# A recurrence on one core: the input quantiser computed in the projection, and matmuls that nobody reads in TensorE's waits

## The reference, cut to what matters

```python
# recurrence, one step a chunk, the state (W_in, W_out) carried on
def step(carry, xs):
    k_h = softmax(einsum('blhd,bDhd->blhD', k_t, W_in)) * lr_t[..., 1:]
    q_h = softmax(einsum('blhd,bDhd->blhD', q_t, W_in))
    o_t = einsum('bqhD,bDhd->bqhd', q_h, W_out) + einsum('bhqk,bkhd->bqhd', qk, v_t)
    W_out = W_out + einsum('bnhD,bnhd->bDhd', k_h, v_t)
    for _ in range(2):            # both states, by attention over the chunk
        ...
# the other way
scale = max(act_scale, 1e-05)
x_int = clip(round(x / scale), -127, 127)
x_dq  = nan_to_num(x_int * scale, nan=0.0, posinf=10000.0, neginf=-10000.0)
y     = einsum('bsi,oi->bso', x_dq, ternary_weight - 1) + bias
```

## Time and profile before

| | us |
|---|---|
| median of 3 runs | 953.45 |
| the 3 runs | 952.24, 953.45, 964.16 |
| the profiled execution | 961.29 |
| its span, first to last instruction | 959.6 |
| mean granted clock of TensorE over the span | 0.784 of 2.4 GHz |

### The profile page before, as it was taken

One profiled execution on the slowest core, in us unless ns is written; L12 is line 12 of the kernel. 1 busy time (PEld: TensorE's weight loads), 2 busy tenths in 40 slices (PEclk: granted clock), 3 DMA queues, 4 the chain that ended last, 5 costly groups with the idle time before them and its releaser, 6 DMA issues. The chain is left out here.

```text
span 959.6 us, 19016 instructions
## 1 busy us (share of the span) xinstructions
PE 674.0 (70%) x6860; PEld 516.7 (54%) x6860; DVE 645.9 (67%) x1809; ACT 341.3 (36%) x794; POOL 377.0 (39%) x513
## 2 busy tenths in 40 slices
PE   1577687788766656899999882154598771696785
PEld 1266465566545535777777682143476551353564
DVE  3763888878857573877777743836554664887886
ACT  1654111111121344666666531211113441475221
POOL 1450444444431454455655055516602662023312
PEclk9988766655669685999999997557757996597895
DMA  2000000000000400120000243364372533100000
GB/s 53 1 1 12 3 2 2 3 2 3 3 2 6 72 0 6 41 77 9 8 8 14 64 132 119 73 97 116 90 179 60 164 108 110 34 0 1 6 17 22
DMA packets 66289, 41.27 MB, mean 43 GB/s; under 512 B 11888, under 2 KB 64192, under 8 KB 66208
## 3 DMA queue, kind: packets, MB, share of 16 engines
q1 hardware_dynamic: 62432, 32.43, 14.2%
q0 software_dynamic: 3776, 7.78, 2.3%
HBM read 26.72 MB, written 13.47 MB: 42 GB/s over the span
## 5 line engine op out<-in xcount | busy, mean ns | idle before, releaser
L1733 ACT ACTIVATE l1a_weights<-l1a_score,l1a_low_top 128x128 f32<-128x128 f32 (+1 forms) x256 | 90.4, 425 | 37.9 <-DVE l1a_low_top L1765 33.9
L1765 DVE TENSOR_REDUCE l1a_low_top<-l1a_score 128x2 f32<-128x512 f32 (+1 forms) x96 | 66.1, 688 | 53.4 <-PE l1a_score L1642 52.4
L1597 POOL TENSOR_TENSOR l1a_q_of<-l1a_q_rows,l_quad_of 128x1024 fp32r<-128x1024 f32 x32 | 59.9, 1895 | 38.0 <-ACT l1a_q_rows L1722 38.0
L1277 POOL DMA_INDIRECT l_done<-l2e_done,l2r_rows x47 | 45.1, 959 | 59.3 <-DVE l2e_done L2482 58.7
L1788 DVE COPY l1a_weightsT<-l1a_flip 128x512 f32<-128x512 f32 x96 | 65.3, 680 | 0.8 <-PE l1a_flip L1677 0.7
L1639 PE MATMUL l1a_score<-l1a_k_rows,l1a_q_of 128*128 128x128 f32 (+1 forms) x256 | 53.2, 313 | 17.9 <-ACT l1a_weights L1733 10.5
L1677 PE MATMUL l1a_flip<-eye,l1a_weights 128*128 128x128 f32 x384 | 59.3, 278 | 0.1
L1639 PEld LDWEIGHTS l1a_score<-l1a_k_rows,l1a_q_of 128*128 128x128 f32 x256 | 38.4, 201 | 33.0 <-ACT l1a_weights L1733 20.5
L1677 PEld LDWEIGHTS l1a_flip<-eye,l1a_weights 128*128 128x128 f32 x384 | 47.4, 145 | 3.1 <-issue 0.8
L827 POOL TENSOR_TENSOR l0s_shared<-l0s_own,l0s_grown 128x512 f32<-128x512 f32 x16 | 18.1, 1132 | 75.3 <-ACT l0s_grown L817 75.3
L1260 POOL DMA_INDIRECT l_rows<-l2r_sent,l2r_slot x32 | 31.9, 998 | 28.6 <-DVE l2r_slot L1244 16.1
(11 more groups left out here) (545 smaller groups left out, 1968.2 us busy)
## 6 DMA issues: line engine op xcount, KB each, us to landing
l2e_wgu<-in_l_wgu SPq DMA_DIRECT2D x47, 128.0 KB, 2.1
l1e_w<-in_l_w SPq DMA_DIRECT2D x46, 128.0 KB, 2.1
l_rows<-l2r_rows SPq DMA_DIRECT2D x1, 3055.0 KB, 19.5
l2e_wd<-in_l_wd SPq DMA_DIRECT2D x47, 64.0 KB, 2.1
l2r_rows<-l_rows SPq DMA_DIRECT2D x3, 780.0 KB, 7.1
l2e_mixed<-l_done SPq DMA_DIRECT2D x8, 256.0 KB, 4.7
l_rows<-l1r_rows SPq DMA_DIRECT2D x1, 1483.5 KB, 11.6
l1r_rows<-l_rows SPq DMA_DIRECT2D x3, 387.0 KB, 3.7
```

What stands on the lines that cost most here:

```text
L1277: self.core.nc.gpsimd.indirect_dma_start(self.done_dram, bass.IndirectOffsetOnAxis(ap=self.rows[:, j, D:D + 1].bitcast(I32), axis=0), done ...
L1597: nc.gpsimd.tensor_tensor(q_of[i][:, 4 * g:4 * g + 4, :], rep(q_rows[:, g, :], 1, 4), rep(lat.quad_of[:, 0, 0:4], 2, L), ALU.mult).then_in ...
L1733: last = nc.scalar.activation(weights[s % 2][:, n * width:(n + 1) * width], score[s % 2][:, n * width:(n + 1) * width], ACT.Exp, bias=low_ ...
L1765: nc.vector.tensor_reduce(low_top[:, s % 2, 0:len(heads)], score[s % 2][:, :].rearrange("p (h k) -> p h k", k=key_tiles * P), AX.X, ALU.ma ...
```

## The change: what it does

The quantiser leaves the scan. `l0_project` gets the scale by a transfer of its own, and VectorE quantises there in four pieces of 512 columns: one after `invert(0)`, one after `invert(1)`, two at the end of its program. In `l0_scan` `quantise` and `choose` are gone, as are the transfer of the scale and the two instructions that prepare it. In the scan's TensorE program `fill` adds ten float32 matmuls to a chunk, 128x128 by 128 columns of `xnT`, into columns of a PSUM bank that no one reads: one at the chunk's head, two ahead of the "own" add, two ahead of the "out" add, one ahead of the scores of "in", and four ahead of the "in" add. The first of them has a new wait, for ScalarE's copy of "grown".

```diff
-def l0_project(core, fast):
+def l0_project(core, fast, act_scale_dram):
...
+            @block.sync
+            def _(sp):
+                sp.dma_start(scale[:, :], act_scale_dram.partition_broadcast(P)).then_inc(scale_in, 16)
...
+                def quantise(c):
+
+                    quant = fast.quant[:, c * CH:(c + 1) * CH]
+                    order.then(nc.vector.tensor_scalar(level[:, :], core.xnT[:, c * CH:(c + 1) * CH], inv[:, :], ROUND, ALU.mult, ALU.add))
+                    order.then(nc.vector.tensor_scalar(level[:, :], level[:, :], -ROUND, LEVELS, ALU.add, ALU.min))
+                    order.mark(nc.vector.tensor_scalar(spare[:, :], level[:, :], -LEVELS, scale[:, :], ALU.max, ALU.mult))
+                    order.then(nc.vector.tensor_scalar(quant, level[:, :], LIMIT, LIMIT, ALU.mult, ALU.min))
+                    order.mark(nc.vector.tensor_scalar(finite[:, :], spare[:, :], 0.0, 0.0, ALU.mult, ALU.is_equal))
+                    order.then(nc.vector.tensor_scalar_max(quant, quant, -LIMIT))
+                    order.then(nc.vector.copy_predicated(quant, finite[:, :], spare[:, :]))
...
                 invert(0)
+                dve.wait_ge(scale_in, 16)
+                order.then(nc.vector.tensor_scalar_max(scale[:, :], scale[:, :], 1e-5))
+                order.then(nc.vector.reciprocal(inv[:, :], scale[:, :]))
+                quantise(0)
                 normalise(0, K)
                 invert(1)
+                quantise(1)
                 normalise(1, Q)
+                quantise(2)
+                quantise(3)
...
+                def fill(count, bank=grown_ps):
+
+                    for _ in range(count):
+                        nc.tensor.matmul(bank[:, 3 * P:4 * P], core.eye[:, :], core.xnT[:, 0:P], start=True, stop=True)
...
                     if c:
+                        pe.wait_ge(grown_kept, c)
+                        fill(1)
                         pe.wait_ge(here_ready, c)
...
                         give_results(c - 1)
+                    fill(2)
                     pe.wait_ge(ready["own"], c + 1)
...
+                    fill(2)
                     pe.wait_ge(ready["out"], c + 1)
...
                     last.then_inc(out_summed, 1)
+                    fill(1)
                     pe.wait_ge(old_ready, c + 1)
...
                     if c < LAST:
+                        fill(4, out_ps)
                         pe.wait_ge(ready["in"], c + 1)
...
-                    quantise(c)
                     dve.wait_ge(out_summed, c + 1)
                     mask(w_old, OLD).then_inc(old_ready, 1)
...
-                    choose(c)
                     if c >= 2:
                         sum_squares(c - 2)
```

More of the change, by code:

```diff
@@ L374, in l0_project @@
         rate_wide = sb("rate_wide", [P, NCK, 8, CK])
+        scale, inv, level, spare = sb("scale", [P, 1]), sb("inv", [P, 1]), sb("level", [P, CH]), sb("spare", [P, CH])
+        finite = local.enter_context(nc.sbuf_tensor("l0p_finite", [P, CH], I32))
+        LEVELS, ROUND, LIMIT = 127.0, 1.5 * 2.0 ** 23, 1e4
         near, far = (local.enter_context(nc.psum_tensor(f"l0p_{n}", [P, BANKS, CH], F32)) for n in ("near", "far"))
@@ L386, in l0_project @@
         norms_drawn, rates_drawn = core.sem("l0p_norms_drawn"), core.sem("l0p_rates_drawn")
-        dve_order, pool_order = core.sem("l0p_dve_order"), core.sem("l0p_pool_order")
+        dve_order, pool_order, scale_in = core.sem("l0p_dve_order"), core.sem("l0p_pool_order"), core.sem("l0p_scale_in")
         def four_chunks(toks, s):
@@ L595, in _, with l0_scan @@
                 invert(0)
+                dve.wait_ge(scale_in, 16)
+                order.then(nc.vector.tensor_scalar_max(scale[:, :], scale[:, :], 1e-5))
+                order.then(nc.vector.reciprocal(inv[:, :], scale[:, :]))
+                quantise(0)
                 normalise(0, K)
                 invert(1)
+                quantise(1)
                 normalise(1, Q)
-def l0_scan(core, fast, w_gate_dram, w_out_dram, ternary_dram, bias_dram, act_scale_dram):
+                quantise(2)
+                quantise(3)
+def l0_scan(core, fast, w_gate_dram, w_out_dram, ternary_dram, bias_dram):
     nc = core.nc
@@ L641, in l0_scan @@
         turned = pair("turned", [P, 2, P])
[L642 to L645, removed]
+        bias, mean, square = sb("bias", [P, D]), sb("mean", [P, H]), sb("square", [P, H, HD])
         w_ps = ps("w", [P, 4, CH])
@@ L667, in l0_scan @@
         dve_order, pool_order = sem("dve_order"), sem("pool_order")
-        tern_in, scale_in, bias_in, later_in = (sem(n) for n in ("tern_in", "scale_in", "bias_in", "later_in"))
+        tern_in, bias_in, later_in = (sem(n) for n in ("tern_in", "bias_in", "later_in"))
         out_done, centred, squared = sem("out_done"), sem("centred"), sem("squared")
@@ L687, in _ @@
             def _(sp):
-                sp.dma_start(scale[:, :], act_scale_dram.partition_broadcast(P)).then_inc(scale_in, 16)
                 sp.dma_start(fast.tern_int[:, :], ternary_dram).then_inc(tern_in, 16)
@@ L889, in mask @@
                                                    rep(rep(fast.w_mask[:, :, :].rearrange("p h i -> p (h i)"), 1, 2), 1, 4), ALU.mult)
[L891 to L903, removed]
                 def centre(c):
@@ L938, in _ @@
                         order.mark(nc.vector.tensor_scalar_add(fast.w_tern[:, :], fast.tern_int[:, :], -1.0))
-                        dve.wait_ge(scale_in, 16)
-                        order.then(nc.vector.tensor_scalar_max(scale[:, :], scale[:, :], 1e-5))
-                        order.then(nc.vector.reciprocal(inv[:, :], scale[:, :]))
                     if c >= 2:
                         centre(c - 2)
-                    quantise(c)
                     dve.wait_ge(out_summed, c + 1)
@@ L3012, in build @@
             layer_norm(core, "l0_norm", core.x, core.xn, core.xnT, LN_EPS, loads=[fast])
-            l0_project(core, fast)
-            l0_scan(core, fast, io["l0_w_gate"], io["l0_w_o"], io["l0_ternary"], io["l0_bias"], io["l0_act_scale"])
+            l0_project(core, fast, io["l0_act_scale"])
+            l0_scan(core, fast, io["l0_w_gate"], io["l0_w_o"], io["l0_ternary"], io["l0_bias"])
             l0_finish(core, fast)
```

## The result

The changed kernel takes 948.07 us in the median of 20 runs (940.79 to 956.23), the kernel before 956.22 beside it (20 runs, 951.11 to 964.16): the ratio is 0.9898, 95% interval 0.9872 to 0.9925. The ratios of this document leave out runs over 1.5% above the fastest of their kernel (here one, 956.23); medians and ranges have all runs. The change gains 1.0%, some 8 to 10 us, where 20 were forecast; 948.07 also lies above the range. The profiled execution is the fastest of the 20, 940.79 us.

The account below looks back on a forecast made before the run. The prediction took the scan to be bound by the loop through the engines, not by one engine. Its sum was 961.3 - 21.4 + 0.9 = 940.8 us for the profiled execution; against the median it took 934, range 926 to 946.

Parts of the forecast that it names:

- I take it that the clock stays at 2.4 GHz through the scan: Scan: the fills' full-array work keeps TensorE's granted clock near 1.00, against 0.61 on the mean before.
- about 10.5: Scan's regular chunks: each falls from 11.84 us to about 10.5, some 19 us in all.
- fast, but with gaps: Scan: rival in which the clock falls in two or three chunks, 4 us each; 941 to 945, chance 0.17.
- slower: Scan: rival in which fills delay awaited matmuls at 1.2 GHz, 2.6 us a slow chunk; about 970, chance 0.05.
- eight slow chunks: Scan: the "slower" rival's count, 8 of 14 chunks slow as now, 21 us on top of 949.
- +0.9: Scan's head: the scan starts 0.9 us later, behind the last two quantiser pieces of the projection.
- last chunk 1.9: Scan's end: D, A and half of "grown" save 0.96 + 0.18 + 0.8 = 1.9 us.
- The projection: Projection: a quantiser piece takes 3.5 us; the first two are hidden, the last two end at 92.5.
- G and A's 5 us less to gain: Scan: faster runs may already have more 2.4 GHz, so gain up to 5 us less, 937 at most.

Follow-up runs that it names:

- fills alone: Kernel before with the ten fills added, quantiser left in the scan: 971.07 us, ratio 1.019 to the kernel before.
- the move alone: Changed kernel without its fills, quantiser in the projection: 954.2 us, ratio 1.000 to the kernel before; cut after layer 1, 316.43 us.
- both changes: Changed kernel with last quantiser piece at the head of the scan and each fill as four 32x32 matmuls: 938.85 us, ratio 0.9797 to the kernel before.
- fills at the barrier: Kernel with both changes, cut after layer 1, plus eight small fills behind the scan's last matmul: 296.54 us against 297.59 without them.
- cut programs: Kernels with layers 2 to 4 left out and the state stored: kernel before 316.39 us, changed kernel 307.27 us.
- last piece moved: Changed kernel with its last quantiser piece moved to the head of the scan's VectorE program: 946.85 us, ratio 0.9886 to the kernel before.
- small fills: Changed kernel with each fill as four 32x32 matmuls side by side: 948.6 us, ratio 0.9877 to the kernel before.

## Why the prediction was wrong

The step that failed is "I take it that the clock stays at 2.4 GHz through the scan", with the two terms that stand on it outside the 14 chunks.

- *The steady chunk, "about 10.5"*: right. Twelve of 14 chunks are 10.49, with each term where it was put: the quantiser's place now ends with TensorE, and the fills at the higher clock delay no awaited matmul. That it is the fills that raise the clock is shown: 0.61 before, it is 0.86 with fills alone and 0.55 to 0.62 with the move alone. That the higher clock pays only with the quantiser out of the way is shown too.
- *The clock in the loop*: the two slow chunks cost 0.75 and 3.0 us. That is the mechanism of the rival "fast, but with gaps", which I gave 0.17 and 941 to 945, at 4 us a slow chunk. The prices of the "slower" rival hold where its condition does: 1.34 us for the fills ahead of "own" and "out", measured 1.5 (3.90 us from the transposed "out" to the mask in the slow chunk, 2.42 with the move alone); 1.30 for the four ahead of "in", measured 1.26 with the fills alone. In the changed kernel's slow chunk that second part is 0.6 (the add could start at 237.91 and starts at 238.53), since the clock rises while the four run. What was wrong is the count of eight slow chunks.
- *The head, "+0.9"*: the start was 0.7 later, as priced, but I costed a later start only, not what TensorE's doubled idle time at the barrier goes with. In six traces with two pieces ahead of the barrier TensorE stands 1.9 us, and in five of them the clock falls 0.6 to 2.5 us behind the scan's first matmul; in the eight others, among them all five with the piece moved behind the barrier, it stands 0.93 and the clock falls 6.2 us or more behind it. Moving the piece thus takes both away; by what path the longer idle time brings the fall is not shown. The first mask is 3.9 us late against 0.2 in the sum: 3.7 lost.
- *The end, "last chunk 1.9"*: it gave 0.8, and `l0_finish`, for which the sum had nothing, took 2.2 us more. In the kernel before the clock is up again at 283, ahead of that stage, and low in it only from 286 to 289 (0.93 over 284 to 307). In the changed kernel it is low from 265 to 279 and again from 286 to 288 (0.80 over 272 to 297.3). The first low stretch, with the matmuls of 512 columns, costs some 0.7 us up to the first gated product; the second costs 1.5, where the product with `w_o` takes 2.84 us, not 2.05. That this loss is the clock's is shown on the kernel with both changes: with fills at the barrier the clock is 1.00 throughout and the stage takes 21.9 us, as in the kernel before.
- *The projection*: right. A piece took 3.3 to 3.4 us (priced 3.5), the first, beside GpSimd's draws, 4.7 and still hidden.
- *The baseline*: the sum was put against a profiled execution and then carried over to the median. The spread between runs, for which I allowed "up to G and A's 5 us less to gain", is hardly the scan's: layer 1 alone spreads over 1.1 us.

Summed on layer 1: 20.5 forecast, less 3.6 in the loop (18.8 against 15.2), 3.7 at the head, 3.3 at the end, is 9.9; measured are 9.8 in the profiled pair, from which the parts are taken, and 9.1 in the cut programs.

## What to carry to other kernels

Price a change that lives on TensorE's clock in three stretches, not one: the steady loop, its entry and its exit, since each barrier at which TensorE idles longer can take back what the loop gained. Test the halves of such a change apart: here the move alone and the fills alone gave 0 and a loss of 1.9%, and the pair gained 1%. When whole runs scatter more than the effect, cut the program behind the changed stage before arguing about a few us.

## What the runs showed of the hardware that was not expected

**A later stage has two speeds.** In seven whole programs layers 2 to 4 took either 641.8 to 641.9 us (changed kernel, last piece moved, both) or 652.1 to 652.5 (the four others), with the same code and nothing between. Nearly all of the difference, 9.7 of 10.7 us in this pair, arises in one place, 400 to 420 us behind the end of layer 1. Windows there, changed kernel, then kernel before:

```profile
697.30:707.30 10.00, 9.89 (x50) 7.31 (x49) 5.78 (x18) 1.12 (x3) 0.00 (x0) 0.90 1.00 243
707.30:717.30 10.00, 7.68 (x43) 6.34 (x41) 4.87 (x19) 5.03 (x13) 1.91 (x2) 0.75 0.15 47
```

```profile
707.10:717.10 10.00, 10.00 (x34) 7.74 (x34) 5.71 (x13) 0.74 (x2) 0.00 (x0) 0.50 1.05 257
717.10:727.10 10.00, 10.00 (x32) 7.24 (x31) 1.96 (x7) 0.74 (x2) 0.00 (x0) 0.50 0.00 0
```

TensorE is busy all of the time at the lower clock and the clock does not rise; in the other execution it has. Of the 20 runs of the changed kernel seven lie at 940.8 to 944.2 and eleven at 946.5 to 951.3, which fits two such speeds; what decides between them was not tried.

**A busy TensorE at 0.50.** The changed kernel's slow chunk has TensorE busy for 10.20 of 10.20 us and a clock of 0.50 throughout, then comes out of it. The chunk ahead of it is like the others to 0.01 us, so what makes the clock fall in one chunk of many stays open. The Trainium skill (TensorE: Matmul & The Clock Gate, What's actually happening) has the gate follow how busy TensorE has been of late; by the traced busy time neither this stretch nor the one above at 10.00 of 10.00 us follows that.

**An instruction stall with small fills.** In the five kernels with small fills the seventh chunk is 10.75 to 11.9 us long; in four of them its "own" add breaks off (both, whole program):

```profile
174.90 0.65 PE L743 MATMUL l0s_w_ps<-l0s_own,l_v_toks 32*128 32x64 f32 x11 [0.50 <-DVE l0s_own L920]
175.94 0.33 PE L743 MATMUL l0s_w_ps<-l0s_own,l_v_toks 32*128 32x64 f32 x3 [0.39 <-issue]
```

Nothing in the profile releases it, and it comes at the same place in the program, whose TensorE has 8092 matmul records where the changed kernel has 7170. That it is the loading of instructions fits, and is not shown: in all four traces a packet of the instruction queue starts 2.5 to 2.7 us ahead of the end of the break, but that queue has one every 3 to 7 us in this part anyway. The break itself is short. What makes the chunk long is that the clock falls 2.3 to 2.8 us behind it in all four; in the fifth kernel, where the add takes 1.07 us without a break, the clock does not fall there and the chunk takes 10.75.
